# Two of four heads' operand copies issued from GpSimd's queue instead of SyncE's, in an attention pass on one core

## The chip, the cores and the metric

One core of a Trainium2 chip runs the whole kernel. Times are device microseconds of that core, the median of several executions. Five engines work side by side, each with its own instruction queue: TensorE (PE), VectorE (DVE), ScalarE (ACT), GpSimd (POOL) and SyncE (SP). They meet through semaphores. A DMA is issued by an instruction in one engine's queue and carried out by 16 DMA engines that all queues share; in the kernel before, SyncE issues every one.

## The reference

Four images of 32 x 32 positions and 384 channels, float32. Each goes through two residual blocks, each on a group-normalised input:

```python
x = x + _L0_conv_ref(_gn(x), ...)   # selective scan in four directions, the first pass
x = x + _L1_conv_ref(_gn(x), ...)   # attention, the second pass
```

The second block is what the change touches:

```python
qkv = (x.reshape(B, L, dim) @ w_qkv + b_qkv).reshape(B, L, 3, nh, hd)   # L = 1024, nh = 12, hd = 32
q, k = rot(q), rot(k)                                # rotary embedding
attn = jnp.einsum('bnqd,bnkd->bnqk', q, k) * scale
rel_h = jnp.einsum('bnhwc,hkc->bnhwk', q6, bias_h)   # relative position by row and by column
rel_w = jnp.einsum('bnhwc,wkc->bnhwk', q6, bias_w)
attn = softmax(attn + rel_h[..., :, None] + rel_w[..., None, :])
out = attn @ v;  return out @ w_proj + b_proj
```

## The kernel before, in words

The kernel has two passes. The first runs the scan of all four images (up to about 1800 us) and leaves the results x1 and their normalised form xn2 in HBM. The second is a hardware loop over the four images (`Fori(0, B)`), about 375 us each, and is what the change touches.

One image of the second pass. The 12 heads are three groups of four (`GROUPS`, `HG`). For each group TensorE projects q and k in halves of 512 positions (`proj`), multiplies by a constant matrix for the rotation (`turn`), and GpSimd and VectorE combine: GpSimd's product with the cosine (L1638), VectorE's with the sine (L1143), GpSimd's sum into QKC (L1645), which raises `rope_ready`. From rotated q TensorE makes the products with the relative positions (`rel`, L824), which VectorE saves to RELC (L1165, `rel_saved`). `PREPARED` is the order in which q and k of the groups are made; their sums are numbered n = 0 to 11, and group 0 has n = 0 to 3.

QKC holds a group's four heads one above the other, 32 partitions each. The score products want each head's operands in another place: QX[:, j] holds for head j q and the relative products twice, KX[:, j] the two halves of k (and a constant). So each head needs six copies from SBUF to SBUF (`HEAD_DMAS`), given by `operands(g, j)`: four of 32 x 1024 elements (128 KB each) and two of 32 x 512. They raise `head_loaded[j]`, 16 a copy.

The steps. A group has 32 steps (`STEPS`): 8 blocks of 128 queries times 4 heads, the heads innermost. Step s of an image runs over groups 0, 1, 2 as s = 0 to 31, 32 to 63 and 64 to 95, and its head is s % 4. In a step TensorE multiplies scores (L851, `s_psum`), VectorE adds the bias and takes the maximum (L1225), ScalarE takes the exponential (L1533), TensorE turns the result around (L862), VectorE or ScalarE saves it (L1179, L1510), and every four steps TensorE weighs the values (L876). TensorE's queue is written two steps of scores ahead.

The copies in time. QX and KX have one place per head. So the copies of group g + 1 for head j can only start once the last scores of head j in group g are done, which is step 28 + j of the group, and they are needed at the first step of head j in the next group, four steps later. SyncE issues them all, head by head, at L523. For the first group the copies are issued at L515 in three portions, q of all heads, then k, then the relative products, as each becomes ready. Behind the last head of group 2 SyncE issues the load of the next image's normalised input (L526), then waits for the output.

At the end of an image each engine tells SyncE that it has left; SyncE clears the semaphores of the image, a contiguous range, and opens the next one.

Of the kernel before, what the change touches and what calls it, by code (L numbers as in the profile page):

```python
# [9 lines left out]
L = IMG * IMG  # L10
CT = C // P
HALF = L // 2
# [5 lines left out]
NH, HD = 12, 32  # L18
HG = P // HD
GROUPS = NH // HG  # L20
QB = L // P
STEPS = QB * HG
HEAD_DMAS = 6
# [79 lines left out]
class Signal:  # L103


    def __init__(self, sem, unit=1):
        self.sem, self.unit = sem, unit

    def after(self, b, n):

        return n * self.unit

    def at(self, n):

# [3 lines left out]
def build(nc, x, mats, cols, sel_in, onehot, b_rows, z_rows, x1, xn2, out):  # L118
    ctx = ExitStack()
    with ctx:  # L120
# [3 lines left out]
        def signal(name, per_image=0, unit=1):  # L124
            return Signal(ctx.enter_context(nc.semaphore(name)), unit)
# [89 lines left out]
        def from_mats(k, n=1):  # L215
            return slots(k if k < 28 else k + 8, n)


        QX = from_mats(19, HG)
        KX = from_mats(23, 2).rearrange("p n l -> p (n l)").rearrange("p (j k) -> p j k", j=HG)  # L220
# [3 lines left out]
        QKC = from_mats(8, 3)  # L224
        RELC = from_mats(30, 4).rearrange("p (g a) l -> p g a l", g=2)
# [58 lines left out]
        dve_a, act_a = signal("dve_a"), signal("act_a")  # L284


        x_loaded = signal("x_loaded", unit=16)
        v_psum = signal("v_psum", QB)
        v_saved = signal("v_saved", QB)
# [5 lines left out]
        rope_ready = signal("rope_ready", 4 * GROUPS)  # L295
        rel_psum = signal("rel_psum", 12)
        rel_saved = signal("rel_saved", 12)
        relw_psum = signal("relw_psum", 2 * GROUPS)
        relw_saved = signal("relw_saved", 2 * GROUPS)
        head_loaded = [signal(f"head{j}_loaded", HEAD_DMAS * GROUPS, 16) for j in range(HG)]  # L300
        s_psum = signal("s_psum", STEPS * GROUPS)
        max_done = signal("max_done", STEPS * GROUPS)
        exp_done = signal("exp_done", STEPS * GROUPS)
# [26 lines left out]
        def leave_image(eng, b):  # L330

            eng.sem_inc(image_done, 1)
            eng.wait_ge(image_open, b + 1)
# [14 lines left out]
        PLACE = {(0, "q"): 0, (0, "k"): 1, (1, "q"): 0, (2, "q"): 2, (1, "k"): 1, (2, "k"): 1}  # L348
# [13 lines left out]
        ROPE_FOR, REL_FOR = [4, 10, 12], [4, 12, 12]  # L362
# [4 lines left out]
        def last_use(n):  # L367
# [6 lines left out]
        LATE = [("sums", 0), ("norm", 0, 0), ("norm", 1, 0), ("sums", 1), ("norm", 0, 1), ("norm", 1, 1),  # L374
                None, None, None, ("sums", 2), ("norm", 2, 0), ("proj", 0, 0), ("proj", 1, 0), ("proj", 2, 0)]
        LATE_AT = {2 * m + 2: job for m, job in enumerate(LATE) if job}

        def norm_count(g, h):

            return 2 * h + g + 1 if g < 2 else 5 + h  # L380
# [11 lines left out]
        def _(sp):  # L392
# [102 lines left out]
            with sp.Fori(0, B) as b:  # L495

                sp.wait_ge(out_stored, 2 * 16 * (b + 1))
                sp.dma_start(X[:, :, :], x1[bass.ds(b, 1), :, :].rearrange("o (k p) l -> p (o k) l", p=P)
                             ).then_inc(x_loaded.sem, 16)

                def operands(g, j):

                    rows = slice(HD * j, HD * j + HD)
                    q, k = QKC[rows, PLACE[g, "q"], :], QKC[rows, PLACE[g, "k"], :]
                    rel = RELC[j::HG, g // 2, 0, :]
                    return [(QX[0:HD, j, :], q), (QX[2 * HD:3 * HD, j, :], q),
                            (KX[0:HD, j, :], k[:, 0:HALF]), (KX[2 * HD:3 * HD, j, :], k[:, HALF:L]),
                            (QX[HD:2 * HD, j, :], rel), (QX[3 * HD:4 * HD, j, :], rel)]


                for k, (ready, count) in enumerate(((rope_ready, 2), (rope_ready, 4), (rel_saved, 2))):
                    sp.wait_ge(ready.sem, ready.after(b, count))
                    for j in range(HG):
                        for dst, src in operands(0, j)[2 * k:2 * k + 2]:
                            sp.dma_start(dst, src).then_inc(head_loaded[j].sem, 16)  # L515
                for g in range(1, GROUPS):
                    sp.wait_ge(rope_ready.sem, rope_ready.after(b, ROPE_FOR[g]))
                    sp.wait_ge(rel_saved.sem, rel_saved.after(b, REL_FOR[g]))
                    for j in range(HG):

                        sp.wait_ge(s_psum.sem, s_psum.after(b, STEPS * g - HG + j + 1))
                        for dst, src in operands(g, j):
                            sp.dma_start(dst, src).then_inc(head_loaded[j].sem, 16)  # L523


                sp.dma_start(XN[:, :, :], xn2[bass.ds((b + 1) % B, 1), :, :].rearrange("o (k p) l -> p (o k) l", p=P)  # L526
                             ).then_inc(normed_loaded, 16)
                for h in range(2):
                    sp.wait_ge(pj_read.sem, pj_read.after(b, CT * (h + 1)))
                    at = slice(h * HALF, (h + 1) * HALF)  # L530
                    sp.dma_start(out[bass.ds(b, 1), :, at].rearrange("o (k p) l -> p (o k) l", p=P), OUT[:, :, at]
                                 ).then_inc(out_stored, 16)

                sp.wait_ge(image_done, 4 * b + 4)
                sp.sem_inc(clearing, 1)
                sp.sem_clear(per_image)
                sp.sem_inc(image_open, 1)
# [6 lines left out]
        def _(pe):  # L544
# [231 lines left out]
            with pe.Fori(0, B) as b:  # L776
# [156 lines left out]
                for s in range(STEPS * GROUPS):  # L933
# [3 lines left out]
                    if k in JOB_AT[g]:  # L937
                        job(g + 1, JOB_AT[g][k])
                    if g + 1 == GROUPS and k in LATE_AT:
                        late(LATE_AT[k])  # L940
                    if s % 2 == 1 and s > HG:
# [21 lines left out]
        def _(dve):  # L963
# [168 lines left out]
            with dve.Fori(0, B) as b:  # L1132
# [101 lines left out]
                for s in range(STEPS * GROUPS):  # L1234
# [4 lines left out]
                    if k - 2 in JOB_AT[g]:  # L1239
                        job(g + 1, JOB_AT[g][k - 2])  # L1240
                    if g + 1 == GROUPS and k - 2 in LATE_AT:
                        late(LATE_AT[k - 2])
                    if g + 1 == GROUPS:
# [302 lines left out]
        def _(pool):  # L1546
# [68 lines left out]
            for b in range(B):  # L1615
                for i in range(ITEMS):
                    n, tile = i % NST, (ITEMS * b + i) // NST + 1
# [13 lines left out]
            pool.wait_ge(att_loaded.sem, att_loaded.at(len(ATT_MATS)))  # L1631

            with pool.Fori(0, B) as b:
                for n in range(2 * len(PREPARED)):
                    tensor, h = divmod(n, 2)
                    at = slice(h * HALF, (h + 1) * HALF)
                    pool.wait_ge(raw_saved.sem, raw_saved.after(b, n + 1))
                    pool.tensor_tensor(RT1[:, h, :], RAW[n if n < 4 else n % 2], W["cos"][:, 0, at], ALU.mult  # L1638
                                       ).then_inc(cos_done.sem, 1)
                    pool.wait_ge(cos_done.sem, cos_done.after(b, n + 1))  # L1640
                    pool.wait_ge(sin_done.sem, sin_done.after(b, n + 1))
                    if n in (4, 10):
                        for loaded in head_loaded:
                            pool.wait_ge(loaded.sem, loaded.after(b, HEAD_DMAS * (1 if n == 4 else 2)))
                    pool.tensor_tensor(QKC[:, PLACE[PREPARED[tensor]], at], RT1[:, h, :], RT2[:, h, :], ALU.add  # L1645
                                       ).then_inc(rope_ready.sem, 1)
                leave_image(pool, b)


# [124 lines left out]
```

## Time and profile before

| | |
|---|---|
| median of 3 runs | 3313.18 us (3310.19 to 3314.7) |
| profiled execution | 3309.41 us, its span 3307.6 us |
| TensorE busy | 2748.0 us, 83% |
| VectorE busy | 2366.0 us, 72% |
| ScalarE busy | 1557.4 us, 47% |
| GpSimd busy | 1335.6 us, 40%, nearly all in the first pass |
| mean granted TensorE clock | 0.948 |

Instructions that issue a DMA do not count as busy. They stand in the timeline and in the chain as SPq, SyncE's queue (and would stand as POOLq, were they GpSimd's). A line such as L851 is a line of the kernel before; the line numbers of the changed kernel are higher by 7 from SyncE's part on.

### The profile page before, as it was taken

What the parts mean: (1) busy time and instruction counts of PE and PEld (TensorE: products, weight loads), DVE (VectorE), ACT (ScalarE), POOL (GpSimd) and SP (SyncE); (2) the same over time, 40 slices, a digit from 0 to 9 for tenths busy, and PEclk for the clock granted to TensorE, in tenths of its full rate; (3) what the DMA queues carried; (4) which work ended last, traced back from release to release, by engine and by line L of the source; (5) the groups of instructions that cost most, each with busy time, mean ns of one, the idle gap of its engine ahead of it and who ended that gap; (6) DMA issues with size and microseconds to landing.
All of it is one profiled execution on the core that took longest, in us unless ns stands there. A gap on an engine that the chain in (4) does not pass through costs nothing. (4 is left out here: it accounts for less than half of the span.)

```text
span 3307.6 us, 40573 instructions
## 1 busy us (share of the span) xinstructions
PE 2748.0 (83%) x15824; PEld 1382.7 (42%) x15824; DVE 2366.0 (72%) x2262; ACT 1557.4 (47%) x1908; POOL 1335.6 (40%) x636
## 2 busy tenths in 40 slices
PE   3577777887678876777667999989998999989999
PEld 1222223332233332222222665556554665555655
DVE  1598899999999999999982466625664356625665
ACT  4445644555435564444431356514563346514564
POOL 4478766887668876766651100011000200011000
PEclk8789998999999999999896999999999999999999
DMA  1334443355443544445541111020111110020110
GB/s 61 128 115 133 153 144 141 130 140 159 145 149 127 140 159 145 161 134 144 182 137 60 30 33 52 1 71 1 33 52 40 33 33 25 29 71 1 33 52 20
DMA packets 93429, 297.51 MB, mean 90 GB/s; under 512 B 15804, under 2 KB 18504, under 8 KB 93224
## 3 DMA queue, kind: packets, MB, share of 16 engines
q1 hardware_dynamic: 93224, 294.73, 28.6%
q8 instruction: 134, 2.20, 0.3%
q14 instruction: 71, 0.58, 0.1%
HBM read 238.57 MB, written 23.07 MB: 79 GB/s over the span
## 5 line engine op out<-in xcount | busy, mean ns | idle before, releaser
L1608 POOL TENSOR_TENSOR arena<-arena 128x1024 f32<-128x1024 f32 x384 | 902.9, 2365 | 325.9 <-DVE arena L1092 277.3
L1092 DVE TENSOR_TENSOR_SCAN arena<-PS,arena 128x1024 f32<-128x1024 f32 x384 | 878.2, 2287 | 86.1 <-ACT PS L1445 62.5
L1445 ACT ACTIVATE PS<-arena,a_inf,a_neg 128x1024 f32<-128x1024 f32 x384 | 463.8, 1208 | 776.8 <-DVE arena L1092 772.4
L564 PE MATMUL PS<-arena,ident 128*128 128x512 f32 x1568 | 804.1, 639 | 19.3 <-ACT arena L1456 15.1
L1225 DVE CUSTOM_DVE_ANT_1 arena<-PS,arena 128x1024 f32<-128x1024 f32 x384 | 467.6, 1219 | 350.4 <-PE PS L851 350.4
L1533 ACT ACTIVATE arena<-arena,neg_max 128x1024 f32<-128x1024 f32 x384 | 441.0, 1149 | 513.4 <-DVE neg_max L1225 513.4
L555 PE MATMUL PS<-arena,sel 96*128 96x512 bf16 x768 | 247.7, 406 | 413.0 <-DVE arena L1100 409.3
L1100 DVE TENSOR_TENSOR arena<-arena,PS 128x1024 f32<-128x1024 f32 x384 | 459.3, 1196 | 9.7 <-PE PS L555 8.9
L564 PEld LDWEIGHTS PS<-arena,ident 128*128 128x128 f32 x1568 | 318.5, 204 | 304.2 <-issue 246.9
L851 PE MATMUL PS<-arena 64*128 64x512 f32 x1536 | 433.1, 641 | 11.1 <-DMA arena<-arena 11.1
L862 PE MATMUL PS<-ident,arena 128*128 128x128 f32 x3072 | 413.9, 278 | 2.6 <-ACT arena L1533 2.6
L1638 POOL TENSOR_TENSOR arena<-arena 128x512 f32<-128x512 f32 x48 | 60.9, 1270 | 837.3 <-ACT arena L1502 837.3
L862 PEld LDWEIGHTS PS<-ident,arena 128*128 128x128 f32 x3072 | 337.6, 141 | 145.7 <-issue 87.9
L555 PEld LDWEIGHTS PS<-arena,sel 96*128 96x128 bf16 x768 | 51.6, 100 | 716.3 <-DVE arena L1100 664.9
L1179 DVE COPY arena<-PS 128x1024 f32<-128x1024 f32 x192 | 233.8, 1218 | 70.0 <-PE PS L862 64.8
L1645 POOL TENSOR_TENSOR arena<-arena 128x512 f32<-128x512 f32 x48 | 61.0, 1271 | 433.2 <-DVE arena L1143 432.3
L1510 ACT ACTIVATE arena<-PS 128x1024 f32<-128x1024 f32 x192 | 193.3, 1007 | 47.2 <-PE PS L862 47.2
L876 PEld LDWEIGHTS PS<-arena 128*32 128x32 f32 x6144 | 157.3, 110 | 128.3 <-issue 118.1
L876 PE MATMUL PS<-arena 128*32 128x128 f32 x6144 | 208.4, 277 | 0.0
L548 PE MATMUL PS<-normed,arena 128*128 128x512 f32 x288 | 143.1, 643 | 22.5 <-issue 21.5
L851 PEld LDWEIGHTS PS<-arena 64*128 64x128 f32 x1536 | 116.3, 184 | 79.1 <-issue 65.2
L824 PEld LDWEIGHTS PS<-arena 128*128 128x128 f32 x1024 | 124.9, 192 | 38.0 <-issue 24.3
(125 smaller groups left out, 2286.2 us busy)
## 6 DMA issues: line engine op xcount, KB each, us to landing
arena<-b_rows SPq DMA_DIRECT2D x256, 512.0 KB, 3.7
arena<-b_rows SPq DMA_DIRECT2D x256, 256.0 KB, 4.0
arena<-arena SPq DMA_DIRECT2D x192, 128.0 KB, 2.9
arena<-arena SPq DMA_DIRECT2D x120, 64.0 KB, 2.0
normed<-xn SPq DMA_DIRECT2D x5, 1536.0 KB, 6.4
normed<-x_in SPq DMA_DIRECT2D x4, 1536.0 KB, 7.9
residual<-x_in SPq DMA_DIRECT2D x4, 1536.0 KB, 8.0
x<-residual SPq DMA_DIRECT2D x4, 1536.0 KB, 6.4
```

The lines of the kernel that those rows point to most:

```text
L555: last = pe.matmul(dst[:, half(h)], lhs, rhs(h), start=(k == 0), stop=(k == len(pairs) - 1))
L564: last = pe.matmul(dst[:, half(h)], lhs, rhs[:, half(h)], start=start, stop=stop, skip_group_check=True)
L851: last = pe.matmul(scores_place(s)[:, h * HALF:(h + 1) * HALF], QX[rows, j, qb * P:(qb + 1) * P], KX[rows, j, :], start=True, stop=True)
L862: last = pe.transpose(turned_place(s)[:, t * P:(t + 1) * P], PR[s % 3][:, t * P:(t + 1) * P], idn)
L876: last = pe.matmul(banks(6, 1)[HD * j:HD * j + HD, (n % 2) * P:(n % 2 + 1) * P], V[:, t, head * HD:(head + 1) * HD], PT[:, n % 2, j, t, :] ...
L1092: dve.tensor_tensor_scan(HS[:, at % 2, ::step], DA[:, ::step], DBU[:, at % R3, ::step], 0.0, ALU.mult, ALU.add).then_inc(scan_done.sem, 1)
L1100: dve.tensor_tensor(HC[:, at % R_HC, :], HS[:, at % 2, :], C_PSUM, ALU.mult).then_inc(hc_ready.sem, 1)
L1179: dve.tensor_copy(PT[:, n % 2, s % HG, :, :], turned_place(s).rearrange("p (t q) -> p t q", t=QB)).then_inc(pt_saved[0].sem, 1)
L1225: dve.tensor_tensor_reduce(out=PR[s % 3].rearrange("p (h w) -> p h w", w=IMG), in0=scores_place(s).rearrange("p (h w) -> p h w", w=IMG), i ...
L1445: act.activation(DA, DELTA[:, tile % 2, :], ACT.Exp, bias=a_inf[:, col:col + 1], scale=a_neg[:, col:col + 1]).then_inc(da_ready.sem, 1)
L1533: act.activation(PR[s % 3], PR[s % 3], ACT.Exp, bias=neg_max[:, s % 4:s % 4 + 1], scale=-1.0, accum_out=row_sum[:, qb, at:at + 1]).then_in ...
L1608: pool.tensor_tensor(DBU[:, at % R3, :], DU[:, tile % 2, :], BSB[:, at % R3, :], ALU.mult).then_inc(dbu_ready.sem, 1)
```

## The change

`operands` moves out of SyncE's loop unchanged. SyncE issues the copies of heads 0 and 1 only. GpSimd issues those of heads 2 and 3, written into its queue behind its own sums: the portion q of group 0 behind sum 1, the portions k and relative products behind sum 3, group 1 behind sum 9 and group 2 behind sum 11. They wait for the same semaphores as before. The semaphores of heads 2 and 3 leave the range that is cleared for each image and count through the whole pass (`kept`), so a wait for them compares with a number that depends on the image.

```diff
-    def __init__(self, sem, unit=1):
-        self.sem, self.unit = sem, unit
+    def __init__(self, sem, unit=1, kept=None):
+        self.sem, self.unit, self.kept = sem, unit, kept
     def after(self, b, n):
-        return n * self.unit
+        return n * self.unit if self.kept is None else (b * self.kept + n) * self.unit
...
+        head_loaded = [None] * (HG // 2) + [
+            Signal(ctx.enter_context(nc.semaphore(f"head{j}_loaded")), 16, HEAD_DMAS * GROUPS) for j in range(HG // 2, HG)]
...
-        head_loaded = [signal(f"head{j}_loaded", HEAD_DMAS * GROUPS, 16) for j in range(HG)]
+        head_loaded[0:HG // 2] = [signal(f"head{j}_loaded", HEAD_DMAS * GROUPS, 16) for j in range(HG // 2)]
...
+        OWN_HEADS = {"sp": range(HG // 2), "pool": range(HG // 2, HG)}
...
                 for k, (ready, count) in enumerate(((rope_ready, 2), (rope_ready, 4), (rel_saved, 2))):
                     sp.wait_ge(ready.sem, ready.after(b, count))
-                    for j in range(HG):
+                    for j in OWN_HEADS["sp"]:
...
-                    for j in range(HG):
+                    for j in OWN_HEADS["sp"]:
                         sp.wait_ge(s_psum.sem, s_psum.after(b, STEPS * g - HG + j + 1))
...
+                def load_first(k):
+                    ready, count = ((rope_ready, 2), (rope_ready, 4), (rel_saved, 2))[k]
+                    pool.wait_ge(ready.sem, ready.after(b, count))
+                    for j in OWN_HEADS["pool"]:
+                        for dst, src in operands(0, j)[2 * k:2 * k + 2]:
+                            pool.dma_start(dst, src).then_inc(head_loaded[j].sem, 16)
+                def load_group(g):
+                    pool.wait_ge(rope_ready.sem, rope_ready.after(b, ROPE_FOR[g]))
+                    pool.wait_ge(rel_saved.sem, rel_saved.after(b, REL_FOR[g]))
+                    for j in OWN_HEADS["pool"]:
+                        pool.wait_ge(s_psum.sem, s_psum.after(b, STEPS * g - HG + j + 1))
+                        for dst, src in operands(g, j):
+                            pool.dma_start(dst, src).then_inc(head_loaded[j].sem, 16)
...
                     pool.tensor_tensor(QKC[:, PLACE[PREPARED[tensor]], at], RT1[:, h, :], RT2[:, h, :], ALU.add
                                        ).then_inc(rope_ready.sem, 1)
+                    if n in (1, 3):
+                        load_first(n // 2)
+                    if n == 3:
+                        load_first(2)
+                    if n in (9, 11):
+                        load_group(1 if n == 9 else 2)
```

SyncE's queue at the boundary from group 1 to group 2, before: four heads of six copies, the first head's wait naming all its conditions, and then the load of the next input (`normed<-xn`); the two heads in the middle are alike.

```order
L523 DMA arena<-arena 32x1024 [waits s_psum]
L523 DMA arena<-arena 32x1024
L523 DMA arena<-arena 32x512 x2
L523 DMA arena<-arena 32x1024 x2
L525 ISA
L526 DMA normed<-xn 128x3x1024
```

The same place in the change. These are the rows behind head 0: the last of SyncE's two heads is head 1, and the input follows it.

```order
L530 DMA arena<-arena 32x1024 [waits s_psum]
L530 DMA arena<-arena 32x1024
L530 DMA arena<-arena 32x512 x2
L530 DMA arena<-arena 32x1024 x2
L533 ISA
L533 DMA normed<-xn 128x3x1024
```

The rows read alike; what moved is their place. Twelve copies stand ahead of the input's load in this boundary where 24 did.

GpSimd's queue from sum 9 (group 1's k) to product 10 in the change; before, the first row is followed directly by the last.

```order
L1668 TENSOR_TENSOR arena<-arena 128x512 [waits sin_done,cos_done]
L1655 DMA arena<-arena 32x1024 [waits s_psum,rel_saved,rope_ready]
L1655 DMA arena<-arena 32x1024
L1655 DMA arena<-arena 32x512 x2
L1655 DMA arena<-arena 32x1024 x2
L1655 DMA arena<-arena 32x1024 [waits s_psum]
L1655 DMA arena<-arena 32x1024
L1655 DMA arena<-arena 32x512 x2
L1655 DMA arena<-arena 32x1024 x2
L1661 TENSOR_TENSOR arena<-arena 128x512 [waits raw_saved]
```

Twelve copies, six for head 2 and six for head 3, came in between two of GpSimd's operations.

GpSimd's queue at the start of an image, from sum 1 on, before.

```order
L1645 TENSOR_TENSOR arena<-arena 128x512 [waits sin_done,cos_done]
L1638 TENSOR_TENSOR arena<-arena 128x512 [waits raw_saved]
L1645 TENSOR_TENSOR arena<-arena 128x512 [waits sin_done,cos_done]
L1638 TENSOR_TENSOR arena<-arena 128x512 [waits raw_saved]
L1645 TENSOR_TENSOR arena<-arena 128x512 [waits sin_done,cos_done]
```

The same in the change.

```order
L1668 TENSOR_TENSOR arena<-arena 128x512 [waits sin_done,cos_done]
L1647 DMA arena<-arena 32x1024 [waits rope_ready]
L1647 DMA arena<-arena 32x1024 x3
L1661 TENSOR_TENSOR arena<-arena 128x512 [waits raw_saved]
L1668 TENSOR_TENSOR arena<-arena 128x512 [waits sin_done,cos_done]
L1661 TENSOR_TENSOR arena<-arena 128x512 [waits raw_saved]
L1668 TENSOR_TENSOR arena<-arena 128x512 [waits sin_done,cos_done]
L1647 DMA arena<-arena 32x512 [waits rope_ready]
L1647 DMA arena<-arena 32x512 x3
L1647 DMA arena<-arena 32x1024 [waits rel_saved]
L1647 DMA arena<-arena 32x1024 x3
```

Four copies of q stand ahead of the two sums of k, and eight more copies behind them. In TensorE's queue one further instruction (an ISA row of line 849) stands in front of the first scores of head 2 in each group.

## Rows read from the trace of the kernel before

**Rows 1.** The page, busy time and the chain that ended last, by engine and line.

```profile
PE 2748.0 (83%) x15824; PEld 1382.7 (42%) x15824; DVE 2366.0 (72%) x2262; ACT 1557.4 (47%) x1908; POOL 1335.6 (40%) x636
...
PE 41%; SPq 4%; issue 1%; DMA 1%; DVE 1%; ACT 0%; POOL 0%; DVEq 0%; POOLq 0%
PE PS L851 11%; PE PS L862 10%; PE PS L548 6%; PE PS L876 5%; SPq L523 4%; PE PS L824 3%; PE PS L783 2%; PE PS L807 1%; PE PS L919 1%; PE PS L905 1%; DMA arena<-arena 1%; PE PS L564 1%; PE PS L896 0%; ACT arena L1533 0%; DVE arena L1225 0%
```

**Rows 2.** Who waited for whom, second pass: total us, times, longest.

```profile
PEld PS L851 <- issue: 65.2, 376, 0.8
...
PE PS L851 <- DMA arena<-arena: 11.1, 12, 1.9
```

**Rows 3.** Busy time by stretch: four images summed, one image, one boundary.

```profile
2175.00:2553.00 378.00, 364.97 (x3176) 219.60 (x3176) 204.63 (x303) 179.91 (x284) 30.18 (x24) 0.99 0.13 35
...
sum 1494.00, PE 1452.00 PEld 875.67 DVE 816.23 ACT 719.24 POOL 119.48; mean PE 363.00 PEld 218.92 DVE 204.06 ACT 179.81 POOL 29.87
...
2423.00:2443.00 20.00, 17.83 (x182) 10.56 (x180) 13.30 (x19) 12.66 (x21) 0.00 (x0) 1.00 0.59 151
```

**Rows 4.** Timeline, group 0 to 1: start, length, engine, line, [idle before].

```profile
2329.20 1.13 PE L851 MATMUL PS<-arena 64*128 64x512 f32 x4
2330.44 16.50 SPq L523 DMA_DIRECT2D arena<-arena  x24
2331.72 1.13 PE L851 MATMUL PS<-arena 64*128 64x512 f32 x4
2335.41 1.13 PE L851 MATMUL PS<-arena 64*128 64x512 f32 x4
2337.92 1.13 PE L851 MATMUL PS<-arena 64*128 64x512 f32 x4
...
2349.95 1.13 PE L851 MATMUL PS<-arena 64*128 64x512 f32 x4 [1.02 <-DMA arena<-arena]
```

**Rows 5.** Timeline, group 1 to 2.

```profile
2423.45 16.31 SPq L523 DMA_DIRECT2D arena<-arena  x24
...
2427.39 1.13 PE L851 MATMUL PS<-arena 64*128 64x512 f32 x4
...
2434.90 1.22 DVE L1179 COPY arena<-PS 128x1024 f32<-128x1024 f32 x1
2436.03 1.21 DVE L1225 CUSTOM_DVE_ANT_1 arena<-PS,arena 128x1024 f32<-128x1024 f32 x1
...
2438.08 1.13 PE L851 MATMUL PS<-arena 64*128 64x512 f32 x4 [0.27 <-DMA arena<-arena]
...
2442.15 1.13 PE L851 MATMUL PS<-arena 64*128 64x512 f32 x4 [1.91 <-DMA arena<-arena]
```

**Rows 6.** One line's instructions, L523: ns min/median/max; its landings.

```profile
L523 SPq DMA_DIRECT2D arena<-arena x192: 540/592/1938, 1951.2 to 3192.3; - x192
...
DMA to landing us min/median/max: 2.0/2.9/4.2
```

**Rows 7.** Timeline of POOL in one image, and its sum's duration.

```profile
2236.17 1.27 POOL L1638 TENSOR_TENSOR arena<-arena 128x512 f32<-128x512 f32 x1 [34.86 <-ACT arena L1502]
...
2326.28 1.28 POOL L1645 TENSOR_TENSOR arena<-arena 128x512 f32<-128x512 f32 x1 [1.59 <-DVE arena L1143]
...
2403.76 1.27 POOL L1645 TENSOR_TENSOR arena<-arena 128x512 f32<-128x512 f32 x1 [8.75 <-DVE arena L1143]
...
L1645 POOL TENSOR_TENSOR arena<-arena x48: 1261/1271/1282, 1813.1 to 3156.7; 128x512 f32<-128x512 f32 x48
```

**Rows 8.** The page, DMA issues of the operand copies: count, KB, us to landing.

```profile
arena<-arena SPq DMA_DIRECT2D x192, 128.0 KB, 2.9
```

**Rows 9.** Timeline, start of an image.

```profile
2194.91 1.26 POOL L1645 TENSOR_TENSOR arena<-arena 128x512 f32<-128x512 f32 x1
2196.20 18.35 SPq L515 DMA_DIRECT2D arena<-arena  x24
2200.05 1.26 POOL L1645 TENSOR_TENSOR arena<-arena 128x512 f32<-128x512 f32 x1
2208.89 0.69 DVE L1165 COPY arena<-PS 128x512 f32<-128x512 f32 x1 [4.75 <-PE PS L824]
2224.62 3.09 PE L851 MATMUL PS<-arena 64*128 64x512 f32 x12
```

**Rows 10.** The next image's input, L526: its issue and register work.

```profile
2439.99 0.40 SPq L526 DMA_DIRECT2D normed<-xn  x1
...
L526 SPq FUSED_REGOPS  x4: 84/84/94, 2060.6 to 3193.0; - x4
L526 SPq MOVE normed<-xn x4: 29/29/29, 2060.7 to 3193.1; - x4
...
DMA to landing us min/median/max: 6.3/6.3/6.9
```

More of the change, by code:

```diff
@@ L376, in build, with operands @@
         LATE_AT = {2 * m + 2: job for m, job in enumerate(LATE) if job}
+        def operands(g, j):
+            rows = slice(HD * j, HD * j + HD)
+            q, k = QKC[rows, PLACE[g, "q"], :], QKC[rows, PLACE[g, "k"], :]
+            rel = RELC[j::HG, g // 2, 0, :]
+            return [(QX[0:HD, j, :], q), (QX[2 * HD:3 * HD, j, :], q),
+                    (KX[0:HD, j, :], k[:, 0:HALF]), (KX[2 * HD:3 * HD, j, :], k[:, HALF:L]),
+                    (QX[HD:2 * HD, j, :], rel), (QX[3 * HD:4 * HD, j, :], rel)]
+        OWN_HEADS = {"sp": range(HG // 2), "pool": range(HG // 2, HG)}
         def norm_count(g, h):
@@ L499, in _ @@
                              ).then_inc(x_loaded.sem, 16)
[L501 to L508, printed above, removed]
                 for k, (ready, count) in enumerate(((rope_ready, 2), (rope_ready, 4), (rel_saved, 2))):
                     sp.wait_ge(ready.sem, ready.after(b, count))
-                    for j in range(HG):
+                    for j in OWN_HEADS["sp"]:
                         for dst, src in operands(0, j)[2 * k:2 * k + 2]:
```

## The prediction

> **What bounds the kernel now.** I read the chain of waits first. The page's chain [rows 1] is TensorE almost all the way (PE 41% of the span, the rest of its pieces cut into small ones), but one entry beside it is not computing: SPq on line 523, 4% of the span. Line 523 is where SyncE issues the copies of a head's operands for groups 1 and 2. A share in the chain is not a price, because the chain only says what came last, so the second view is who waited for whom in the second pass [rows 2]. TensorE waited for a DMA in front of the score products (L851) 12 times, 11.1 us in all, 1.9 us at the longest. That is the whole price of the late copies in all four images, 0.34% of 3307.6 us. Everything else in that list is DVE, ACT and POOL waiting for one another while TensorE works; the pass is bound by TensorE, busy 1452 of 1494 us in the four images [rows 3].
>
> Third, the timeline at the two group boundaries of one image. Group 0 to 1 [rows 4]: the score products of steps 28 to 31, the last of the group, start at 2329.20, 2331.72, 2335.41 and 2337.92. SyncE starts right behind the first of them (2329.20 + 1.13 = 2330.33 for its end, 2330.44 for the issue, so 0.11 us of reaction) and then issues 24 copies in one unbroken piece of 16.50 us, 0.69 us each. It is behind from the second head on: the heads come free in about 9 us and it needs 16.5. Steps 32 to 34 start without a wait; step 35, head 3, waits 1.02 us. Group 1 to 2 [rows 5] is the same with tighter steps: 24 copies in 16.31 us, step 66 (head 2) waits 0.27 us and step 67 (head 3) 1.91 us. The other images repeat this: 12 waits are 4 images times one at the first boundary and two at the second.
>
> A copy of head operands takes a median 2.9 us from the start of its issue to landing, 2.0 to 4.2 [rows 6]. Check: the last of the 24 is issued near 2439.2 and step 67 starts at 2442.15.
>
> **The change, part by part.** Let p be the time in which POOL issues one copy. A copy on SyncE lands 2.9 us after its issue starts, of which 0.69 is the issue, so I put one from POOL at 2.2 + p, and 12 in a row at 12p + 2.2 from the first issue to the last landing; the reaction of 0.11 I keep.
>
> *Removed from SyncE:* 12 of 24 copies at each boundary. Heads 0 and 1 are then through 12 x 0.69 = 8.3 us after release. They did not wait before, and gain nothing.
>
> *Added to POOL at the boundaries.* POOL is empty there: its last sum of the group is at 2326.28 before the first boundary and at 2403.76 before the second [rows 7], so the queue stands at the wait. Head 2 is released when step 30 ends: 2335.41 + 1.13 + 0.11 = 2336.65. Head 3 is released at 2339.16, while POOL still issues head 2. Step 35 could start at 2349.95 - 1.02 = 2348.93, so the window is 12.3 us. At the second boundary it opens at 2427.39 + 1.13 + 0.11 = 2428.63; step 67 could start, with both waits gone, at 2442.15 - 1.91 - 0.27 = 2439.97, so 11.3 us. The wait that replaces the old one is therefore 12p + 2.2 less 12.3, or less 11.3. Over four images:
> change = 4 x max(12p - 10.1, 0) + 4 x max(12p - 9.1, 0) - 11.1 us.
> Head 2 alone needs 6p + 2.2 within 9.2 us (step 66 at 2437.81), which holds to p = 1.17, and beyond that its wait is part of head 3's, since the same row of 12 ends later.
>
> *The size of p.* No DMA of this trace is issued by POOL; all of them read SPq [rows 6, 8]. Bounds by the nearest rows: from below SyncE's 0.69 us for the very same copy, from above the shortest thing that POOL does here, a 128x512 sum, 1.27 us [rows 7], since a copy issued by POOL is one more job of an engine that takes over a microsecond for any. Below 0.69 I see no reason. By row the nearer one is POOL's, the same engine, so I take 1.05, a little above the middle. Then 12p + 2.2 = 14.8, and the change is 4 x 2.5 + 4 x 3.5 - 11.1 = +12.9 us. At 0.69 it is 0 + 0 - 11.1 = -11.1; at 1.27 it is 4 x 5.1 + 4 x 6.1 - 11.1 = +33.9. It is zero at p = 0.92.
>
> The Trainium skill, "DMA: Bandwidth & Descriptors", section "Latency and other measured facts", gives about 600 ns to the first byte for a DMA from the SP or ACT queue and about 1 us for one from GpSimd. No run here shows the second figure. If those 0.4 us fall on each issue, an estimate by that page is p = 1.09 and +17 us; if they fall on the latency alone, p stays 0.69 and the sum is -11.1 us.
>
> *At the start of an image* [rows 9]. SyncE issued 24 copies from 2196.20, in 18.35 us. Now POOL, after its second sum (2196.17), issues four copies of q before it goes on to k. Its last sum of k ends at 2201.31 and moves to 2201.3 + 4p. Who waits for it: SyncE's copies of k, and nothing of TensorE before step 0 (its relative-position products need only the first two sums). Then four copies of k and, once the first two copies of the relative products are done (2208.89 + 0.69), four more. With p = 1.05 POOL ends near 2213.9, the last lands at 2216.1; head 2 is wanted at step 2, near 2226.7, since L851 begins at 2224.62. That leaves 10 us, so this is hidden. The cover is gone where 2201.3 + 12p + 2.2 passes 2226.7, at p = 1.93. POOL's own next job comes at 2236.17 [rows 7].
>
> *The counters.* The two moved semaphores are not cleared per image, so their waits compare with a register. TensorE gets one more instruction in front of heads 2 and 3, three times an image, 12 in all; DVE and POOL get two each an image, on engines that idle. SyncE's register work costs 84 and 29 ns [rows 10], so 12 x 0.11 = 1.3 us. Bounds: 0, and 12 x 0.8 us, the longest gap of issue in front of L851 [rows 2], = 9.6.
>
> *The next image's input* [rows 10]. SyncE issues it at 2439.99, behind its 24 copies; now it follows 12, near 2431.8, and takes 6.3 us, until 2438.1. It used to meet nothing; now it shares the DMA engines with POOL's copies. With p = 1.05 POOL issues the last ones after 2438 and they meet free engines: 0. With p near 0.69 it meets them all: the input holds about 0.8 of the engines' time for those 6 us, so up to 1 to 2 us of the 2.2 gained at each second boundary goes back, 4 to 8 us.
>
> Sum: +12.9 + 1.3 = +14.2 us against the profiled execution (3309.41 us, span 3307.6). The median of the three runs is 3313.18; the same difference on it gives 3327.4.
>
> **The rivals.**
> *A, POOL issues as fast as SyncE* (p up to 0.8). For it: the copies and engines are the same, and POOL is busy 30 of 375 us of an image [rows 3]. Against it: nothing POOL does here is shorter than 1.26 us. Result: -11.1 + 1.3 = -9.8, or 3303, less what the input takes back, to about 3310.
> *B, break-even* (p from 0.8 to 0.95): the old wait of SyncE is replaced by one of POOL of the same size. -7.8 to +4.6 us; 3313.
> *C, POOL is far slower, and slower still while DVE works* (p over 1.35). One mechanism: each copy needs several pieces of work inside POOL that must reach SBUF. By the sum, p = 1.5 gives 4 x 7.9 + 4 x 8.9 - 11.1 + 1.3 = +57 us, 3370; past 1.93 the image start adds to it. In the 20 us of the second boundary DVE is busy 13.3 [rows 3], with copies and score operations of 1.22 us [rows 5]. If POOL could not write during them, about two thirds of its issues would be held back by half of one, 0.4 us each: p near 1.45, 3366. Those DVE rows take 1.2 ns an element, one element a cycle at best, which speaks against a mode that locks anything. The Trainium skill, "SBUF — State Buffer", section "SBUF: two separate sides", states such a lock: a DMA from GpSimd starves while DVE runs a two-port mode, as an fp32 copy from SBUF to SBUF does. Here DVE's copies read PSUM, so by that rule it should not bite; no row shows it either way.
> *D, the change does not do what it says:* the heads wait for something other than issue. Against it stand the unbroken 24 issues of rows 4 and 5, and the last issue plus 2.9 us falling on the start of step 67. I give it nothing of its own.
>
> **How the numbers follow.** The forecast (p 0.95 to 1.35, +4.6 to +43 us) 0.45; A 0.15; B 0.20; C 0.20. A measurement of this kernel can tell 0.2%, 6.6 us, from no change. Faster by more: most of A and a little of B, 0.14. Within: B, the part of A that the input takes back, and the edge of the forecast below p = 0.97, 0.27. Slower: the rest, 0.59. The range reaches down to A's full gain, 3303, and up to p = 1.5, 3370; outside are the upper part of C and little else. The likeliest case alone is 3318 to 3356.
>
> **What would show it.** POOL's queue has rows of its own for 12 copies at each boundary; their spacing is p, the number on which all hangs. L851's waits for DMA are fewer but longer: one or two a boundary, near 2.5 and 3.5 us, 24 us in all instead of 11.1, and the chain shows POOLq where SPq stood. Heads 0 and 1 wait for nothing. At the image start L851 begins as before. The input's issue stands 8 us earlier. I am wrong if the waits vanish (p under 0.8), if they grow past 6 us each (C), or if the start of an image moves.

## The result, and the profile after

| | before | changed |
|---|---|---|
| median | 3310.15 us (8 runs) | 3322.01 us (8 runs) |
| range | 3303.71 to 3314.70 | 3318.55 to 3325.54 |
| profiled execution | 3309.41 us, span 3307.6 | 3321.7 us, span 3319.9 |

The ratio is 1.0036, 95% interval 1.0025 to 1.0047: 12 us slower, where 14 were forecast. Run again beside other kernels (below) the ratio was 1.0019 (1.0010 to 1.0028), 6 us. Slower is sure; the size is some 6 to 12 us.

The number came out, but not for the reason that was given. First the page after, where it answers to [rows 1] and [rows 8].

```profile
PE 2762.4 (83%) x15824; PEld 1388.3 (42%) x15824; DVE 2364.9 (71%) x2262; ACT 1557.2 (47%) x1908; POOL 1410.2 (42%) x780
...
q0 software_dynamic: 6144, 15.74, 2.1%
...
PE 44%; DMA 1%; POOL 1%; issue 1%; DVE 1%; ACT 0%; SPq 0%; POOLq 0%; DVEq 0%
...
arena<-arena SPq DMA_DIRECT2D x96, 128.0 KB, 3.0
arena<-arena POOLq DMA_DIRECT2D x96, 128.0 KB, 4.2
normed<-xn SPq DMA_DIRECT2D x5, 1536.0 KB, 11.9
```

The change did what it says: 144 more instructions on POOL, a second DMA queue, SPq down to 0% of the chain. GpSimd's issues count as busy and stand as POOL, not as POOLq, as the section on the profile before had expected; and the lines of GpSimd's part are higher by 23, not by 7 (L1645 is now L1668). GpSimd's copies take 4.2 us to land where SyncE's take 3.0, and the next image's input takes 11.9 us where it took 6.4. Next, who waited for whom in the second pass (us, times, longest), against [rows 2].

```profile
PE PS L858 <- DMA arena<-arena: 17.3, 9, 3.7
...
POOL arena L1655 <- issue: 4.5, 1, 4.5
```

These are 17.3 us of waits in front of the score products (now L858), where 11.1 stood. The second row is GpSimd's queue standing still once; it comes back in the last section. The lines of GpSimd's copies of groups 1 and 2, min/median/max in ns, answer to [rows 6]:

```profile
L1655 POOL DMA_DIRECT2D arena<-arena x96: 499/504/568, 1962.5 to 3200.2; - x96
...
DMA to landing us min/median/max: 1.8/3.8/10.3
```

An issue on GpSimd takes 0.50 us (12 in 6.18, so 0.515 each), less than SyncE's 0.68. So the pace on which the forecast rested is half of what was assumed. The timeline shows what happened. Group 0 to 1 of image 2, against [rows 4]:

```profile
2334.97 8.48 SPq L530 DMA_DIRECT2D arena<-arena  x12
...
2341.66 6.18 POOL L1655 DMA_DIRECT2D arena<-arena  x12 [9.58 <-PE PS L858]
...
2353.39 1.13 PE L858 MATMUL PS<-arena 64*128 64x512 f32 x4
```

The last row is step 35, which no longer waits. Group 1 to 2 of the same image, against [rows 5]:

```profile
2426.88 7.53 SPq L530 DMA_DIRECT2D arena<-arena  x12
...
2432.56 6.18 POOL L1655 DMA_DIRECT2D arena<-arena  x12 [24.09 <-PE PS L858]
...
2434.65 0.63 SPq L533 DMA_DIRECT2D normed<-xn  x1
...
2442.57 1.13 PE L858 MATMUL PS<-arena 64*128 64x512 f32 x4 [1.31 <-DMA arena<-arena]
...
2446.89 1.13 PE L858 MATMUL PS<-arena 64*128 64x512 f32 x4 [2.16 <-DMA arena<-arena]
```

SyncE, free after 12 copies, issues the next image's input at 2434.65, 2 us after GpSimd has begun. Steps 66 and 67 (heads 2 and 3) wait for 1.31 and 2.16 us. The chain of waits in this stretch says what step 67 waited for (start, length, what):

```profile
2432.56 4.94 POOL arena L1655 x10
...
2438.20 8.64 DMA arena<-arena
```

The last copy is issued at 2438.20, early enough, and lands 8.64 us later. These are the landings of GpSimd's copies in the first and the second boundary of this image, and the input's:

```profile
DMA to landing us min/median/max: 2.6/3.4/3.7
...
DMA to landing us min/median/max: 2.4/7.7/8.6
...
DMA to landing us min/median/max: 11.7/11.7/11.7
```

While heads 2 and 3 wait, the DMA engines are busy all the time. The row gives a stretch in us, then busy time and count of PE, PEld, DVE, ACT, POOL, then the granted clock, the DMA share (1.01, where 0.59 stood over the 20 us of this boundary in [rows 3]) and GB/s:

```profile
2440.00:2444.00 4.00, 2.69 (x25) 1.53 (x16) 0.95 (x3) 2.32 (x4) 0.00 (x0) 1.00 1.01 290
```

The two second-boundary waits of images 1, 3 and 4 sum to 3.61, 5.12 and 3.75 us. Of the 17.3 us only 1.3 lie elsewhere, in image 4, right behind the standstill of GpSimd's queue.

One more loss shows in the busy times by stretch. Image 3 waits longest, 3.71 us; these are 6 us from just before its end:

```profile
2826.00:2829.00 3.00, 2.20 (x8) 0.70 (x12) 0.07 (x1) 0.00 (x0) 0.00 (x0) 0.50 0.00 1
2829.00:2832.00 3.00, 3.00 (x38) 2.52 (x32) 1.16 (x2) 1.24 (x2) 0.00 (x0) 0.50 0.00 0
```

TensorE's granted clock is at the lower of its two levels, 1.2 instead of 2.4 GHz, and the four score products take 2.08 us instead of 1.13. So a long wait can be paid twice. It isn't always: over the 16 us from step 66 on, the mean clocks of images 1 to 4 are 0.89, 1.00, 0.79, 1.00 after and 0.89, 1.00, 1.00, 0.89 before, though TensorE waits in all eight of these second boundaries. One less the clock, times 16 us, gives 5.1 us after and 3.5 before. The difference of 1.6 us is not clear of chance: two kernels below that leave all copies on SyncE (the counters alone, and the control) also come to 5.1 us, with three stretches of 0.89 each.

### The profile page after: what moved, and what is told of

It reads as the page before. It is cut to its first block and busy times, and to the rows that moved or that the text cites. A ratio compares the mean times of both kernels' runs of the same rounds, so it can differ in the third digit from the quotient of the medians.

```text
span 3319.9 us, 40609 instructions
## 1 busy us (share of the span) xinstructions
PE 2762.4 (83%) x15824; PEld 1388.3 (42%) x15824; DVE 2364.9 (71%) x2262; ACT 1557.2 (47%) x1908; POOL 1410.2 (42%) x780
## 5 line engine op out<-in xcount | busy, mean ns | idle before, releaser
L571 PE MATMUL PS<-arena,ident 128*128 128x512 f32 x1568 | 814.1, 646 | 20.2 <-ACT arena L1463 15.5
L858 PE MATMUL PS<-arena 64*128 64x512 f32 x1536 | 434.4, 643 | 17.3 <-DMA arena<-arena 17.3
L1668 POOL TENSOR_TENSOR arena<-arena 128x512 f32<-128x512 f32 x48 | 61.0, 1270 | 432.9 <-DVE arena L1150 432.0
L555 PE MATMUL PS<-normed,arena 128*128 128x512 f32 x288 | 143.8, 645 | 22.5 <-issue 21.5
L858 PEld LDWEIGHTS PS<-arena 64*128 64x128 f32 x1536 | 116.8, 185 | 85.0 <-issue 65.6
## 6 DMA issues: line engine op xcount, KB each, us to landing
normed<-xn SPq DMA_DIRECT2D x5, 1536.0 KB, 11.9
```

The costliest lines, as they stand in the source:

```text
L555: last = pe.matmul(dst, lhs, rhs(h), start=(k == 0), stop=(k == len(pairs) - 1))
L571: last = pe.matmul(dst[:, half(h)], lhs, rhs[:, half(h)], start=start, stop=stop, skip_group_check=True)
L858: last = pe.matmul(scores_place(s)[:, h * HALF:(h + 1) * HALF], QX[rows, j, qb * P:(qb + 1) * P], KX[rows, j, :], start=True, stop=True)
```

## The experiments

Theory 1: the input's load, moved ahead by SyncE's shorter queue, holds the DMA engines while GpSimd's copies need them. Theory 2: copies on GpSimd's queue are slow in themselves. Ratios are to the kernel before, run again beside the others: 3312.6 us beside the first four kernels, 3315.25 beside the last four.

**The input held back.**

```diff
+                for j in OWN_HEADS["pool"]:
+                    sp.wait_ge(head_loaded[j].sem, head_loaded[j].after(b, HEAD_DMAS * GROUPS))
                 sp.dma_start(XN[:, :, :], xn2[...])
```

> The change, with one wait more: SyncE issues the next image's input only when all copies of heads 2 and 3 have landed. Theory 1 (the input's load, moved ahead by the shorter queue of SyncE, takes the DMA engines from GpSimd's copies): at the boundary from group 1 to 2 the waits of TensorE for these copies, 15.9 us in eight waits, fall to under 2 us, the copies issued by GpSimd there land in about 3.4 us (median) instead of 7.7, the input lands in about 6.3 us instead of 11.7, and the kernel takes 16 us less than the changed one, about 3306, which is 8 us less than before (ratio 0.997 to 0.998). Theory 2 (copies issued by GpSimd are slow in themselves): landings stay over 6 us, waits stay over 12 us, time stays within 4 us of 3322.

Measured: 3299.55 us, ratio 0.9957 (0.9944 to 0.9971), 13 to 14 us less than before, more than the 8 us that theory 1 had said. Its waits:

```profile
POOL arena L1657 <- issue: 4.0, 1, 4.0
...
PE PS L860 <- DMA arena<-arena: 0.8, 1, 0.8
```

and its second boundary, with GpSimd's copies as before and the input behind them:

```profile
2422.61 7.52 SPq L530 DMA_DIRECT2D arena<-arena  x12
...
2428.29 6.18 POOL L1657 DMA_DIRECT2D arena<-arena  x12 [24.09 <-PE PS L860]
...
2438.20 0.40 SPq L535 DMA_DIRECT2D normed<-xn  x1
2439.00 1.13 PE L860 MATMUL PS<-arena 64*128 64x512 f32 x4
```

GpSimd's copies land there in 3.3 us (median), where they took 7.7, and the input in 6.3, where it took 11.7:

```profile
DMA to landing us min/median/max: 2.4/3.3/4.0
...
DMA to landing us min/median/max: 6.3/6.3/6.4
```

The row of 16 us from step 66 on in image 3 has TensorE busy throughout at full clock:

```profile
2811.00:2827.00 16.00, 16.00 (x172) 9.60 (x170) 12.59 (x19) 9.48 (x17) 0.00 (x0) 1.00 0.27 99
```

Theory 1 holds, theory 2 falls. The rows of the other three images are alike, so the clock's 3.5 us of before are gained too: 10.3 us of waits and 3.5 of clock are 13.8. The spans counted from SyncE's first copy of group 1 in image 1 to the end say the same: 1356.5 us before (3307.6 - 1951.15), 1364.1 changed (3319.9 - 1955.77), 1342.6 here (3298.4 - 1955.76): -13.8. That these agree to a tenth is chance: in the two kernels below whose time is that of before (the counters alone, the control) the same span is 1356.9 and 1360.4 us, so it is good to some 4 us.

**The same collision without GpSimd.**

```diff
                         for dst, src in operands(g, j):
                             sp.dma_start(dst, src).then_inc(head_loaded[j].sem, 16)
+                        if (g, j) == (GROUPS - 1, HG // 2 - 1):
+                            sp.dma_start(XN[:, :, :], xn2[...]).then_inc(normed_loaded, 16)
-                sp.dma_start(XN[:, :, :], xn2[...]).then_inc(normed_loaded, 16)
```

> The kernel before, all copies on SyncE, with the input's load moved ahead of the copies of heads 2 and 3 of group 2. Theory 1: the collision does not need GpSimd; the copies behind the input land in 5 us or more instead of 2.9, the waits of TensorE at that boundary grow from 8.8 us to about 20, the kernel takes 8 to 14 us more than before, about 3321. Theory 2 (only GpSimd's copies suffer): one issue of 0.4 us is added to a queue that is late by as much, 4 x 0.4 = 1.6 us, no measurable change.

Measured: 3329.91 us, ratio 1.0050 (1.0036 to 1.0064), 17 us more than before, somewhat over the expectation of theory 1; the profiled execution, 3334.9 us, was the slowest of its five. Image 2, and the landings of the 12 copies behind the input there:

```profile
2440.98 0.40 SPq L525 DMA_DIRECT2D normed<-xn  x1
2441.42 8.30 SPq L523 DMA_DIRECT2D arena<-arena  x12
...
2452.56 2.08 PE L852 MATMUL PS<-arena 64*128 64x512 f32 x4 [4.97 <-DMA arena<-arena]
...
DMA to landing us min/median/max: 3.7/5.6/8.0
```

All its waits:

```profile
PE PS L852 <- DMA arena<-arena: 22.6, 7, 6.0
```

On one queue the copies stand behind the input outright and land in 5.6 us instead of 2.9 (medians of this boundary). The clock is 0.79 in all four images, 13.4 us by the measure above. Waits and clock together are 21.4 us over before, the second pass from its first boundary on only 18.6 longer; the sum of the two is thus good to some 3 us.

The Trainium skill, "DMA: Bandwidth & Descriptors", section "Issuing engines are not separate DMA queues", says that DMAs of all issuing engines run on the same 16 DMA engines and interleave. The trace agrees: copies that meet the input land later from either queue, 7.7 and 5.6 us against 3.3 and 2.9.

**The counters alone.** All copies on SyncE (`OWN_HEADS = {"sp": range(HG), "pool": range(0)}`, GpSimd's calls left out), the two semaphores still kept.

> The change without GpSimd's queue: all copies on SyncE again, but the semaphores of heads 2 and 3 keep counting and are waited for against a register. This is the price of the counters alone. My sum has 1.3 us (12 instructions on TensorE at 0.11 us), bounds 0 and 9.6: ratio 1.000 to 1.001, waits for DMA as before, 11 us in 12 waits. The rival (the counters explain the part of the 12 us that the waits of TensorE do not, about 6 us): ratio 1.002.

Measured: 3314.46 us, ratio 1.0006 (0.9997 to 1.0015), no difference; waits 9.4 us in ten, a little under the 11 us in twelve of before. The register work of TensorE's queue has two rows:

```profile
L849 PEldq FUSED_REGOPS  x12: 37/37/51, 1852.5 to 3195.7; - x12
L849 PEldq EVENT_SEMAPHORE  x4: 51/51/51, 1847.7 to 2981.6; - x4
```

That is 0.65 us in all. Its span from the first copy of group 1 is 1356.9 us (3314.1 - 1957.20), 0.4 over before.

**The input between groups 1 and 2.**

```diff
+                    if g == 2:
+                        sp.wait_ge(proj_psum.sem, proj_psum.after(b, 4 * GROUPS))
+                        sp.dma_start(XN[:, :, :], xn2[...]).then_inc(normed_loaded, 16)
```

> The change with the input's load issued earlier still, between the copies of groups 1 and 2, as soon as the last projection has read the old input; no copy is near it there. Theory 1: as in the run with the load held back, waits at the second boundary under 2 us, time 16 us less than the changed kernel, about 3306, ratio to before 0.997 to 0.998. Theory 2: no change against the changed kernel, 3322. If holding the load back helps and this does not, the load's own place matters in another way.

Measured: 3299.86 us, ratio 0.9960 (0.9947 to 0.9974), as good as holding it back. Its waits:

```profile
PE PS L860 <- DMA arena<-arena: 1.4, 2, 1.2
```

**The changed kernel again.**

> The changed kernel itself once more, beside the kernel before and the three others of this group on one chip, so that they can be set against each other. If the accounting of the second pass is right (6.2 us more of waits and 1.7 us from one more stretch of low clock), the median lies 8 us above before, ratio 1.0024; 1.0036 was measured. If something outside these stretches costs as much again, it comes out at 1.0036 or more again, and the second pass's span from the first boundary on is over 10 us longer than in before.

Measured: 3321.06 us, ratio 1.0019 (1.0010 to 1.0028); waits 15.6 us in nine, second pass from the first boundary 1363.9 us (3319.2 - 1955.32). The accounting of 8 us is inside the interval, so no further cost is needed to explain the time. How much of the 8 us is clock remains open, by what was said above of the stretches at 0.89.

**All copies on GpSimd.** The same, with `"sp": range(0), "pool": range(HG)` and all four semaphores kept.

> All four heads' copies on GpSimd's queue, none on SyncE's, the input's load between groups 1 and 2. 24 copies at 0.515 us take 12.4 us where SyncE took 16.3. Head 3's last copy is issued 0.6 + 11.8 us after the release of head 0 and lands 3.5 us later, 15.9 us, where step 67 could start 16.5 us after it. Theory 1 (issue pace and free DMA engines decide, not the number of queues): under 3 us of waits for DMA in all, time as with the load between and two queues, ratio 0.996. Rival (two queues are needed, the second path is slower): waits over 8 us, ratio 0.999 or above. In the three kernels with 144 copies on GpSimd its queue stood still for 4.0 to 4.5 us before copy 129; here there are 72 an image, so the same should fall on the boundary from group 1 to 2 of image 2 and again near copy 257, in image 4, with a wait of TensorE of 1 to 4 us each.

Measured: 3301.02 us, ratio 0.9960 (0.9947 to 0.9974). A second queue isn't needed: GpSimd's pace is enough. Its waits, then its second boundary in image 1, unbroken, and in image 2, where the queue stood still for 2.17 us:

```profile
PE PS L859 <- DMA arena<-arena: 2.9, 5, 1.6
...
2046.78 12.31 POOL L1656 DMA_DIRECT2D arena<-arena  x24 [18.91 <-PE PS L859]
...
2420.13 4.12 POOL L1656 DMA_DIRECT2D arena<-arena  x8 [18.90 <-PE PS L859]
2426.43 8.20 POOL L1656 DMA_DIRECT2D arena<-arena  x16 [2.17 <-issue]
```

The queue stood still before copy 129, as expected, and once more before copy 243 instead of 257. All five waits stand in the two boundaries in which it did.

**Head 3 alone on GpSimd.** `"sp": range(HG - 1), "pool": range(HG - 1, HG)`, only head 3's semaphore kept, the input between.

> Only head 3 on GpSimd's queue, heads 0 to 2 on SyncE's, the input's load between groups 1 and 2. SyncE's 18 copies take 12.4 us, head 2's last lands near its step (0.3 us late at worst, four times); head 3 has 9 us of slack. GpSimd issues 72 copies in all, fewer than 128, so its queue does not stand still. Waits for DMA under 2 us in all, ratio 0.996 as with two heads on each, perhaps 1 us better. If the gain needs half of the copies moved, it falls to half, ratio 0.998.

Measured: 3314.06 us, ratio 0.9999 (0.9989 to 1.0008). A miss: no gain at all. (The profiled execution, 3320.16 us, was the slowest of its eleven.) The second boundary of image 2, then all waits:

```profile
2430.35 13.45 SPq L534 DMA_DIRECT2D arena<-arena  x18
...
2438.11 3.12 POOL L1657 DMA_DIRECT2D arena<-arena  x6 [26.17 <-PE PS L860]
...
2446.67 2.08 PE L860 MATMUL PS<-arena 64*128 64x512 f32 x4 [1.94 <-DMA arena<-arena]
...
PE PS L860 <- DMA arena<-arena: 11.7, 8, 2.3
```

The step that waits is 66, head 2, which stayed with SyncE. SyncE needs 0.75 us a copy here (13.45 / 18), and 0.79 to 0.85 at the first boundaries (14.22 and 15.21 us), against 0.68 before: its last copy is issued near 2443.1. Eight waits sum to 11.7 us, about as before the change. I had taken SyncE's pace as fixed. In this boundary its first 12 copies, ahead of GpSimd's, took 7.75 us to issue, 0.65 each, and the last six, beside them, 5.7 us, 0.95 each; the input's issue in the change, also beside GpSimd's copies, took 0.60 us (median) where it took 0.40 in the kernel with the input held back. So SyncE's issues are slower while GpSimd's copies are in flight; by what, no run separates.

**Control, all on SyncE, the input between.**

> Control: the kernel before, all copies on SyncE, with the input's load moved between the copies of groups 1 and 2, as in the fast variant. In before no copy is behind the load at the boundary, so by theory 1 nothing is gained: 12 waits, 11 us, ratio 0.999 to 1.001. If the load's place gives the gain by itself, without GpSimd, the ratio is 0.996.

Measured: 3315.27 us, ratio 0.9999 (0.9990 to 1.0008). The load's place is worth nothing by itself; it must only not meet the copies.

```profile
PE PS L853 <- DMA arena<-arena: 12.4, 12, 1.9
```

The three fastest are the change with the input held back, with the input between the groups, and all copies on GpSimd: 13 to 14 us under the kernel before, each ratio within the others' intervals, and by the ratios 20 to 26 us under the change.

## Why the prediction was right in sign and size, and wrong in mechanism

*What bounds the kernel.* Right in the main. The late copies cost 11.1 us of waits; the 3.5 us of low clock behind some of them were not in the price. Without the waits the kernel gains 13 to 14 us, not 11. And one reading of the list of waits was wrong: not all else in it is other engines waiting for one another. TensorE also stands still for 7.2 us at the start of each of three images (21.5 us) and for 6.8 us in four waits in front of L919. The change leaves both as they were, so the sum doesn't suffer.

```profile
PE PS L548 <- issue: 21.5, 3, 7.2
...
PE PS L919 <- DVE arena L1196: 6.8, 4, 1.7
```

*The pace p.* Wrong: this is the step that failed. I took 1.05 us, from SyncE's 0.69 below and GpSimd's shortest operation, 1.27, above, and excluded less than 0.69. It is 0.515. GpSimd's shortest operation, the reason for going above SyncE's pace, had nothing to do with how fast it issues. With 0.515 the term of GpSimd's 12 copies, +24 us in the sum, is zero, as the run with the input held back shows (one wait of 0.8 us left, behind the standstill). The prediction had named a p under 0.8 as the sign of being wrong. (At p = 1.27 its formula gives +34.0, not +33.9; nothing hangs on it.)

*The landing.* Taken as 2.2 + p, so 2.7 at the real pace; measured 3.3 without a collision, and 0.6 us of reaction instead of 0.11 (in the change, 2432.56 against 2430.83 + 1.13). Too small to matter: 0.6 + 11 x 0.515 + 3.3 = 9.6 us lie inside the window of 11.3. The Trainium skill, "DMA: Bandwidth & Descriptors", section "Latency and other measured facts", gives about 1 us to the first byte for GpSimd's path and about 0.6 for SyncE's, an estimate of 0.4 us for the difference. From the start of an issue to landing the traces have the same difference (3.3 to 2.9); the reaction adds another 0.5. It fell on the latency, not on each issue: the second of the two readings given in the prediction, though p did not stay at 0.69 either.

*The input.* Seen and placed rightly (8.8 us earlier, counted from SyncE's first copy of the boundary), and mis-sized; this is the second failed step. At the forecast it had 0, in rival A 4 to 8 us. Between the change and the change with the input held back lie 21.5 us (1364.1 - 1342.6): 16.5 of waits and 5.1 of clock. The reasoning let the input finish in its 6.3 us and left the rest of the engines' time to the copies; in fact all end late, the input after 11.7 us and GpSimd's copies after 7.7. That the DMA engines are what they share is borne out by their share of 1.01, and not tested by itself.

*The rivals.* A was the true mechanism up to the collision: waits gone at the first boundary, but for the 1.3 us behind the standstill, and, with the input out of the way, at the second. C did not happen: GpSimd's issues at the boundaries took 499 to 568 ns with VectorE at work beside them. The lock of which the Trainium skill, "SBUF — State Buffer", section "SBUF: two separate sides", tells did not show, in line with its own condition. D is excluded by the run with the input held back.

*The start of an image and the counters.* Right: from SyncE's first copy of an image to its first copy of group 1 image 2 takes 134.24 us before (2330.44 - 2196.20) and after (2334.97 - 2200.73), and the counters cost 0.65 us instead of 1.3.

So the two errors, +24 us for a pace that is not slow and 0 for a collision worth 21.5, cancelled. That the sum came out was luck; the mechanism that it stood for did not happen. The first pass, which the change does not touch, adds noise: SyncE's first copy of group 1 (GpSimd's, where it has them all) came anywhere from 1951.15 to 1958.03 us in the ten profiles, 1951.15 in before's and 1955.77 in the change's, and that explains 4.6 of the 12.3 us between the two profiled executions.

## What to carry to other kernels

When work leaves a queue, look at what stood behind it there: it now starts earlier, and if it is a large DMA it can meet the very transfers that were to be made faster. Give such a load a condition of its own instead of its place in a queue. The price of a wait is not only the wait: after some of the long ones TensorE came back at half clock. In the three fastest kernels the medians fell by 13 to 14 us, the waits only by 8.2 to 10.3 from the 11.1 of before.

## What was not expected of the hardware

Issuing one of these copies from GpSimd took 0.50 us, less than the 0.59 us median on SyncE; SyncE's own issues became slower beside GpSimd's copies, 0.95 us apart instead of 0.65.

GpSimd's queue stood still once, with nothing to wait for in the profile, in front of its 129th copy, in all four traces with 144 copies (4.5, 4.0, 4.4 and 3.9 us) and in the one with 288 (2.2 us, and 2.8 before the 243rd); with 72 copies it never did. Here is the changed kernel:

```profile
3102.24 4.11 POOL L1655 DMA_DIRECT2D arena<-arena  x8 [9.57 <-PE PS L858]
...
3110.88 2.07 POOL L1655 DMA_DIRECT2D arena<-arena  x4 [4.53 <-issue]
```

It cost TensorE 1.3 us here, and 0.8 and 1.2 us in the kernels with the input held back and with the input between the groups. What the queue waits for stays open; the second standstill came after 114 more copies, not after 128, so a count of copies alone doesn't give it.
